# A DLRM tower on one core: ten gathers a chunk in the order of DRAM rows, one transfer out of them, and weights loaded in another order

## The reference, cut to what matters

```python
e = jnp.stack([tbl_0[ids[:, 0]], ..., tbl_38[ids[:, 38]]], axis=1)     # 512 x 39 x 16
z0 = einsum('bid,bjd->bdij', e, e).reshape(B, D, 39 * 39)
cur0 = relu(einsum('bdk,kl->bld', z0, W0))                             # W0: 1521 x 128
next_h, direct0 = split(cur0, 2, axis=1)                               # 64 each
z1 = einsum('bid,bjd->bdij', e, next_h).reshape(B, D, 39 * 64)
cur1 = relu(einsum('bdk,kl->bld', z1, W1))                             # W1: 2496 x 128
z = sum(concatenate([direct0, cur1], axis=1), axis=-1)                 # 512 x 192
h = concatenate([z, dense_ctx], axis=1)                                # 512 x 208
h = maximum(h @ W_top1 + b_top1, 0)
h = maximum(h @ W_top2 + b_top2, 0)
y = h @ W_top3
```

## Time and profile before

| | us |
|---|---|
| median of 3 runs | 443.81 (440.96 to 448.94) |
| profiled execution, its own time | 441.91 |
| its span in the profile | 439.9 |
| matmul busy | 407.8 (93%) |
| VectorE busy | 347.9 (79%) |
| GpSimd busy | 285.5 (65%) |
| ScalarE busy | 225.7 (51%) |

### The profile page before, as it was taken

How to read it: one execution, slowest core, us unless ns; L and a number is a source line. 1 busy time by engine, 2 the same in 40 slices (tenths; PEclk the granted TensorE clock), 3 DMA queues, 4 the chain that set the end, 5 groups by cost and what they waited for, 6 DMA issues and landing times.

```text
span 439.9 us, 4140 instructions
## 1 busy us (share of the span) xinstructions
PE 407.8 (93%) x1490; PEld 250.4 (57%) x1490; DVE 347.9 (79%) x196; ACT 225.7 (51%) x224; POOL 285.5 (65%) x180
## 2 busy tenths in 40 slices
PE   0578699899999999999999999999999999996997
PEld 0444356446566656565756565666656565664564
DVE  0203755799999998989898989898989898999700
ACT  3114345365565647483747474747383747462422
POOL 5787878888888888888888888888888100000000
PEclk9989799999999999999999999999999999999899
DMA  8373629696959495959595977777786858570000
GB/s 282 97 180 76 133 62 217 155 208 153 213 116 213 111 208 112 212 110 216 108 220 120 200 142 171 157 178 153 176 165 157 180 138 197 127 161 0 1 0 2
DMA packets 23988, 64.03 MB, mean 146 GB/s; under 512 B 6755, under 2 KB 14904, under 8 KB 17695
## 3 DMA queue, kind: packets, MB, share of 16 engines
q1 hardware_dynamic: 17620, 60.75, 61.7%
q0 software_dynamic: 5632, 1.35, 3.1%
q10 hardware_dynamic: 715, 1.66, 1.1%
HBM read 59.88 MB, written 3.85 MB: 145 GB/s over the span
## 4 chain that ended last, share of the span: by engine, by line
PE 76%; POOL 12%; issue 5%; DVE 3%; DMA 3%; ACT 0%; DVEq 0%
PE acc L487 15%; POOL found L266 12%; PE acc L519 12%; PE acc L512 11%; PE acc L511 11%; PE acc L530 9%; PE sums L470 6%; PE acc L526 4%; PE spread L500 3%; DVE z_lo L409 3%; DMA found<-in_table_dram,rows_sb 2%; PE spread L559 2%; PE sums L550 1%; DVE z L401 1%; DMA base_sb<-in_base_dram 1%
## 5 line engine op out<-in xcount | busy, mean ns | idle before, releaser
L266 POOL DMA_INDIRECT found<-in_table_dram,rows_sb x176 | 285.3, 1621 | 56.7 <-issue 53.3
L309 ACT ACTIVATE z_hi<-z 128x2048 fp32r<-128x2048 f32 x64 | 122.4, 1912 | 83.1 <-DVE z L401 78.4
L409 DVE TENSOR_TENSOR z_lo<-z,z_hi 128x2048 fp32r<-128x2048 f32 x64 | 146.2, 2286 | 14.6 <-ACT z_hi L309 8.8
L487 PE MATMUL acc<-squares,w 128*128 128x512 f32 (+1 forms) x224 | 111.2, 614 | 0.0
L511 PE MATMUL acc<-z_hi,w_hi 128*128 128x512 f32 x256 | 106.2, 415 | 4.5 <-issue 2.3
L401 DVE TENSOR_TENSOR z<-x_wide,h 128x2048 f32<-128x2048 f32 x48 | 109.6, 2283 | 0.0
L512 PE MATMUL acc<-z_hi,w_lo 128*128 128x512 f32 x256 | 100.2, 391 | 0.0
L401 DVE TENSOR_TENSOR z<-spread,h 128x2048 f32<-128x2048 f32 x32 | 73.2, 2286 | 20.8 <-issue 17.0
L285 ACT ACTIVATE squares<-sums 128x1024 f32<-128x1024 f32 x64 | 58.4, 913 | 59.7 <-PE sums L470 45.7
L519 PE MATMUL acc<-z_lo,w_hi 128*128 128x512 f32 x256 | 83.3, 447 | 1.8 <-DVE z_lo L409 1.8
L519 PEld LDWEIGHTS acc<-z_lo,w_hi 128*128 128x128 f32 x256 | 48.5, 191 | 26.2 <-issue 15.1
(11 more groups left out here) (44 smaller groups left out, 144.5 us busy)
## 6 DMA issues: line engine op xcount, KB each, us to landing
x_wide<-x_rows SPq DMA_DIRECT2D x96, 512.0 KB
x_parts<-x_rows SPq DMA_DIRECT2D x32, 128.0 KB
found<-in_table_dram,rows_sb POOLq DMA_INDIRECT x176
x_rows<-found SPq DMA_DIRECT2D x32, 80.4 KB
w_sb<-in_w_dram SPq DMA_DIRECT2D x1, 1280.0 KB, 6.8
x_rows<-found SPq DMA_DIRECT2D x16, 73.1 KB
z<-in_select_dram ACTq DMA_DIRECT2D x1, 576.0 KB, 7.5
wt_sb<-in_wt_dram SPq DMA_DIRECT2D x1, 512.0 KB
```

The lines of the kernel that those rows point to most:

```text
L266: pool.indirect_dma_start(out=found[:, b, 2, s * D:s * D + D], out_offset=None, in_=table, in_offset=bass.IndirectOffsetOnAxis(ap=rows_sb[ ...
L309: nc.scalar.activation(z_hi[:, n % RING], z[:, n % RING], ACT.Copy).then_inc(hi_done, 1)
L409: nc.vector.tensor_tensor(z_lo[:, n % RING], z[:, n % RING], z_hi[:, n % RING], ALU.subtract).then_inc(lo_done, 1)
L487: last = nc.tensor.matmul(acc0[:, :], w0[rows, t, :], squares[rows, q % RING0, a, :], start=(t == 0), stop=(t == T0 - 1))
```

## The change

The gathered rows are numbered field by field: row f * 32 + b of a chunk, 1248 in all, lies in partition (f * 32 + b) // 10, column (f * 32 + b) % 10. So ten gathers of 125 partitions hold a chunk (GP = 125, SLOTS = 10 for each chunk), and the 125 partitions lie one behind another in DRAM, so that one transfer lays them out. The base values become a table as large as the indices'. Sizes of chunks become lists (SIZES, WIDTH, START), all at their old values. SP loads w0a and mix, which ScalarE's queue did; ScalarE's queue loads w1, which SP's did; the last layers' weights are loaded behind chunk 5's layout. `split(0)` on VectorE stands ahead of w0's sum, on ScalarE ahead of w1's high part; `split(1)` stands ahead of `evict0(0)` on ScalarE and ahead of `multiply(0)` on VectorE. TensorE runs 14 and 5 matmuls of `keep_busy` around the mix instead of 30 behind it, and 12 instead of 14 later; one wait of the dense layers names an earlier multiply.

```diff
-CB = 32
-SETS = 3
-GP = SETS * F
-SLOTS = -(-CB // SETS)
+SIZES = [32] * 16
+GP = 125
+SLOTS = [-(-F * size // GP) for size in SIZES]
+SLOT0 = [sum(SLOTS[:c]) for c in range(CHUNKS)]
...
-        base_sb = sb("base_sb", [GP, 1])
+        base_sb = sb("base_sb", [GP, sum(SLOTS)], I32)
...
             def lay_out(c):
-                b = c % BUFS
+                b, w = c % BUFS, SLOTS[c] * D
                 sp.wait_ge(found_lo_done, c + 1)
-                for s, w in enumerate(SET_COLS):
-                    start = x_rows[b, 0, 0, GW * s:GW * s + 1]
-                    sp.dma_start(bass.AP(start.tensor, start.offset, [[N, F], [FR * N, 3], [1, w]]),
-                                 found[F * s:F * s + F, b, :, 0:w]).then_inc(rows_out[b], 16)
+                start = x_rows[b, 0, 0:1]
+                sp.dma_start(bass.AP(start.tensor, start.offset, [[w, GP], [FR * N, 3], [1, w]]),
+                             found[:, b, :, 0:w]).then_inc(rows_out[b], 16)
...
             sp.dma_start(ids_sb[:, :], ids).then_inc(ids_in, 16)
-            sp.dma_start(w1_sb[:, :, :], w1).then_inc(w1_in, 16)
-            for dst, src in LAYERS:
-                sp.dma_start(dst, src).then_inc(mlp_in, 16)
+            sp.dma_start(w0[:, :, :], w0a).then_inc(w0_in, 16)
+            sp.dma_start(mix_sb[:, :, :], mix).then_inc(mix_in, 16)
             sp.wait_ge(filler_in, 16)
...
                 if c + BUFS < CHUNKS:
                     bring(c + BUFS)
+                if c == 2:
+                    for dst, src in LAYERS:
+                        sp.dma_start(dst, src).then_inc(mlp_in, 16)
...
-                for s in range(SLOTS):
+                for s in range(SLOTS[c]):
+                    i = SLOT0[c] + s
                     pool.indirect_dma_start(
...
-            act.dma_start(w0[:, :, :], w0a).then_inc(w0_in, 16)
             act.dma_start(w0b_sb, w0b).then_inc(w0_in, 16)
-            act.dma_start(mix_sb[:, :, :], mix).then_inc(mix_in, 16)
+            act.dma_start(w1_sb[:, :, :], w1).then_inc(w1_in, 16)
             act.wait_ge(select_in_done, 16)
...
+            split(0)
             act.wait_ge(w1_in, 16)
             nc.scalar.activation(w1_hi[:, :, :], w1_sb[:, 0:VT, :], ACT.Copy).then_inc(w1_hi_ready, 1)
-            split(0)
             for d in range(ND):
                 square(d)
+            split(1)
             evict0(0)
-            split(1)
...
-            nc.vector.tensor_scalar(rows_sb[:, :], ids_sb[:, :], base_sb[:, 0:1], None,
-                                    ALU.add).then_inc(rows_ready, 1)
+            nc.vector.tensor_tensor(rows_sb[:, :], ids_sb[:, :], base_sb[:, :], ALU.add).then_inc(rows_ready, 1)
+            split(0)
             dve.wait_ge(w0_in, 32)
...
             nc.vector.tensor_copy(w0[0:F, 0, :], acc1[0:F, 0:P]).then_inc(w0_ready, 1)
-            split(0)
             dve.wait_ge(w1_hi_ready, 1)
...
             dve.wait_ge(select_ready, 1)
+            split(1)
             multiply(0)
-            split(1)
...
                 if m == 3 and batch == early:
-                    pe.wait_ge(multiplied, G * CHUNKS)
+                    pe.wait_ge(multiplied, G * (CHUNKS - 1) + SPREAD[-1] + 1)
...
+            pe.wait_ge(select_ready, 1)
+            keep_busy(acc0, 14)
             pe.wait_ge(w0_ready, 1)
             pe.wait_ge(mix_in, 16)
...
             last.then_inc(mixed, 1)
-            pe.wait_ge(select_ready, 1)
-            keep_busy(acc0, 30)
+            keep_busy(acc0, 5)
             add_up(0)
...
-            keep_busy(acc1, 14)
+            keep_busy(acc1, 12)
```

More of the change, by code:

```diff
@@ L20 @@
 HALF = 64
-CB = 32
-N = CB * D
-CHUNKS = B // CB
-SETS = 3
-GP = SETS * F
-SLOTS = -(-CB // SETS)
-GW = SLOTS * D
-SET_COLS = [GW, GW, N - 2 * GW]
+SIZES = [32] * 16
+CHUNKS = len(SIZES)
+START = [sum(SIZES[:c]) for c in range(CHUNKS)]
+WIDTH = [size * D for size in SIZES]
+N = max(WIDTH)
+GP = 125
+SLOTS = [-(-F * size // GP) for size in SIZES]
+SLOT0 = [sum(SLOTS[:c]) for c in range(CHUNKS)]
+GW = max(SLOTS) * D
 DENSE = 16
@@ L189, in uses, with gathers @@
             return c // BUFS + 1
+        def gathers(c):
+            return sum(SLOTS[c % BUFS:c + 1:BUFS])
         block = ctx.enter_context(nc.Block())
@@ L469, in add_up @@
                 for a, t in enumerate(DUOS[q % ND]):
-                    last = nc.tensor.matmul(sums[:, a, :], select_sb[:, t, :], x_parts[:, c % BUFS, :],
+                    last = nc.tensor.matmul(sums[:, a, 0:w], select_sb[:, t, :], x_parts[:, c % BUFS, 0:w],
                                             start=True, stop=True)
@@ L486, in contract0 @@
                 for a, t in enumerate(DUOS[d]):
-                    last = nc.tensor.matmul(acc0[:, :], w0[rows, t, :], squares[rows, q % RING0, a, :],
+                    last = nc.tensor.matmul(acc0[:, 0:w], w0[rows, t, :], squares[rows, q % RING0, a, 0:w],
                                             start=(t == 0), stop=(t == T0 - 1))
@@ L499, in spread_out @@
                     rows = slice(32 * q, 32 * q + 32)
-                    last = nc.tensor.matmul(spread[:, q, :], select_sb[rows, T0 + i, :], x_parts[rows, c % BUFS, :],
+                    last = nc.tensor.matmul(spread[:, q, 0:w], select_sb[rows, T0 + i, :], x_parts[rows, c % BUFS, 0:w],
                                             start=True, stop=True)
@@ L631, in layout @@
     tables = [np.ascontiguousarray(inputs[f"tbl_{f}"]) for f in range(F)]
-    by_set = np.zeros((SETS, F, CHUNKS, SLOTS), np.int32)
-    for s, cols in enumerate(SET_COLS):
-        w = cols // D
-        rows = ids.reshape(CHUNKS, CB, F)[:, s * SLOTS:s * SLOTS + w]
-        by_set[s, :, :, 0:w] = rows.transpose(2, 0, 1)
-    starts = np.cumsum([0] + [t.shape[0] for t in tables])[:F].astype(np.float32)
+    starts = np.cumsum([0] + [t.shape[0] for t in tables])[:F].astype(np.int32)
+    by_slot, base = np.zeros((2, GP, sum(SLOTS)), np.int32)
+    for c, size in enumerate(SIZES):
+        cols = slice(SLOT0[c], SLOT0[c] + SLOTS[c])
+        flat, flat_base = np.zeros((2, GP * SLOTS[c]), np.int32)
+        flat[0:F * size] = ids[START[c]:START[c] + size].T.reshape(-1)
+        flat_base[0:F * size] = np.repeat(starts, size)
+        by_slot[:, cols] = flat.reshape(GP, SLOTS[c])
+        base[:, cols] = flat_base.reshape(GP, SLOTS[c])
     from_w0 = np.asarray(inputs["L0_rec_W0"]).reshape(F, F, P)
@@ L676, in layout @@
     return {
[L677 to L678 removed]
+        "ids": by_slot,
+        "base": base,
         "table": np.concatenate(tables),
```

113 lines of the change are left out of this document (61 added, 52 removed).

## The result

The changed kernel takes **444.74 us** (median of 20 runs, 442.31 to 447.81) against 441.87 for the kernel before in the same session (20 runs, 439.83 to 457.15): ratio 1.0081, 95% interval 1.0057 to 1.0104. That is within 2%, but the interval lies above 1: slower, and not faster as forecast. The profiled execution took 444.69 us with a span of 442.8, 2.9 more than before. Executions that ran disturbed (such as the 457.15 of the kernel before) are left out of every ratio, so a ratio is not quite the quotient of the two medians.

The account below looks back on a forecast made before the run. TensorE's matmuls were taken to bound the kernel at 22.88 us a chunk, with only the start movable. TensorE's chain gained 5.9 us, but chunk 3's gathers decided: 442.9 - 4.3 = 438.6 us, range 431.5 to 445.5.

Parts of the forecast that it names:

- Indices: Loads of row numbers and base values at the start: two large loads instead of one and a tiny one, +0.8 us.
- Gathers of chunk 0: GpSimd's gathers at the start: one fewer (-1.30) and w0's sum no longer slowing one (-0.77), -2.07 us.
- Transfer out: Chunk 0's rows sent out after its split: one transfer instead of three, +0.6 us between bounds -0.85 and +2.05.
- h: Chunk 0's h, which allows the first multiply: 0.8 - 2.07 + 0.6 = -0.7 us, first multiply at 39.1.
- The clock and the idle time: TensorE around chunk 1's sums: 2.13 us of idle time and 3.1 us of low clock go, together -5.2 us.
- TensorE's chain: TensorE's work by the time of chunk 2's split: -0.7 - 5.2 = -5.9 us.
- Chunk 2's split: Its gathers land at 50 to 53.5 against a split at 53.5: no wait, but no slack.
- Chunk 3's gathers: Late next, and deciding: landing moves by -4.3 us, ScalarE waits about 6 us ahead of the split, not 4.85.
- A: Rival: index loads and transfer out spread over fewer DMA engines, both upper bounds hold (+2.4, +2.05); 441.7 us, chance 0.26.
- B: Rival: the wait ahead of chunk 3's split goes too, ten gathers landing before ScalarE asks; 433.7 us, chance 0.21.
- C: Rival: fewer warming matmuls let a low clock come elsewhere, so the 3.1 us are lost; 440.2 us, chance 0.12.
- D: Rival: the transfer out goes through so few DMA engines that it bounds every chunk; 486 us, chance 0.04.

Follow-up runs that it names:

- the version with wide loads: The changed kernel with its index and base loads and its transfer out each cut in 120 and 5 partitions, gathers still of 125: 442.89 us, ratio 1.0035.

## Why the prediction was wrong

**The step that failed** is "That 125 rows cost more than 117 would add at most 7% of 10.0 us, 0.7; the row is 1.00 whatever is beside it, so I take 0." The price was bounded by the number of rows, and then put at nothing. It was 1.21 us, 21% more, and does not go by the rows. The prediction had the rule that fits in its hand. The Trainium skill, page "DMA: Bandwidth & Descriptors", section "Why a DMA increments its semaphore by 16 and not by 1", takes the largest number up to 16 that divides the outer dimension on both sides; by it 128, 126, 117, 125, 115 and 127 partitions go to 16, 14, 13, 5, 5 and 1 engines. The issues measured 0.95, 1.00, 1.00, 1.21, 1.19 and 2.55 us: the fewer engines, the longer, and the transfers out likewise. By the same rule each engine gets 8, 9, 9, 25, 23 and 127 rows of a gather, and 0.88 us plus 0.013 us for each of these rows, an estimate fitted to the measured times, meets all six within 0.04 us. The section has an exception for some direct copies that GpSimd issues, 16 engines for any count; the gathers, which are indirect, did not show it, since by it 127 partitions would have cost what 128 do. No trace shows the DMA engines one by one, so that the price goes by this number rests on the six counts. In the prediction the rule was applied to the loads and the transfer out, but not to the gathers, the only ones of which there are 160.

**Step by step.**

- *Indices:* +0.8 forecast, +1.66 measured, within its bounds. At the end it was worth about 1.5 us with 126 partitions, and in the changed kernel, together with the transfer out, up to 2 us by the medians and nothing in the trace (the version with wide loads).
- *Gathers of chunk 0:* -2.07 forecast; from the first issue to the split it is 16.53 us against 16.37, +0.16.
- *Transfer out:* +0.6 forecast, +1.35 measured, within its bounds, and free.
- *h:* -0.7 forecast. The split that h now waits behind came at 42.15, not 37, since its gathers were late, and the first multiply was at 43.74, not 39.1. "Cost 0, cover about 1 us" failed with the cover, by the price of ten more gathers; 1.3 us of it is the split's place (42.40 with it back).
- *The clock and the idle time:* half right. TensorE had no idle time ahead of chunk 1's sums, and from the second sum over that chunk (53.40) to the spread (57.96) it was 4.56 us instead of 7.49, 2.9 gained against 3.1 forecast. But a low stretch came earlier instead, behind the 5.47 us of idle time that end at 48.12, and from the first multiply (+3.9) to chunk 0's whole group (+0.2) 3.7 us were gained, not 5.2.
- *TensorE's chain:* -5.9 forecast, +0.2 measured, h's +3.9 less the 3.7. ScalarE was to reach chunk 3's split at 68.7 and reached it at 74.75, and chunk 1's wide transfers, put 5.3 us earlier, were issued at 65.50, 1.4 later than in the earlier trace rows. With 126 partitions both were nearly met (69.47, and 58.71). This second miss need not have cost anything: the gathers landed 8.9 us after ScalarE was there.
- *Chunk 2's split:* no wait, as forecast.
- *Chunk 3's gathers:* rightly named as what decides. The fortieth's issue was to end at 67.7 to 68.1 and ended at 75.45: 0.9 of it the indices, about 4.8 the price of the 39 before it (67.33 us for them, 62.5 forecast), 1.7 its own slow issue, held up by VectorE. The landing was to move by -4.3 and moved by +4.47.
- *Last layers' loads, w0's and w1's order, the tail, the period:* nothing, as forecast. The steps stay at 22.86 across the last layers' loads (issued from 134.62).

**The rivals.** A, narrow transfers, was the right rule in two harmless places: with both of its prices real the forecast of 441.7 still missed the third. B's second stall grew instead. C's mechanism came, a low stretch elsewhere; with 126 partitions doing away with it gave 0.75 us at chunk 1's whole group. D's mechanism shows with 127 partitions, one engine by the rule (17.92 us out to place in chunk 0, and the largest part of the chain), not with 125. The range, to 445.5, held the time only because of A's margin. What the change's idea is worth with a fitting number shows at 126: 1.3% less, near the forecast's 1.0% (438.6 against 442.9). That is in part luck, since there the indices and the transfer out cost nothing (+0.03 and -0.18 us, not +0.8 and +0.6).

## What to carry to other kernels

Choose the number of partitions of a gather, a load or a transfer out for its divisors before its rows: 126 in place of 125 was worth 9 us here, 7 of them by the gathers, and 127, one run, cost 270. Where two chains meet at one wait (here TensorE's and GpSimd's at chunk 3's split), work out both arrival times; what the earlier one gains is only idle time. Such a price is to be measured with one row of the very shape, not bounded by its size.

## What the runs showed of the hardware

VectorE's operations that read two operands from SBUF hold GpSimd's gathers up: an issue of 1.00 us takes 4.69 beside two of them and 9.09 beside four, and stays at 1.00 beside one that reads an operand from PSUM (78.94 above). Where the gathers fall among them changes with small shifts. The changed kernel with the transfer out in two had its fortieth gather issued at 71.70 without such a hold-up and landed at 80.70 in its profiled execution, 2.9 us ahead of the changed kernel's, though the price of its gathers is the same. So a few us between two profiled executions at this place prove little by themselves.

The last step, from chunk 14's whole group to chunk 15's, was about 21.9 or 23.5 us in all kernels but one (25.3 with 126 partitions and chunk 3's split later). TensorE idles for a part of it (busy 1.81 us in 404 to 408 in the kernel before), and in some the granted clock falls behind that. The kernel before (step 23.47), and the same with chunk 1's split ahead (21.88), in 408 to 412:

```profile
408.00:412.00 4.00, 4.00 (x8) 1.82 (x6) 4.00 (x3) 2.92 (x2) 0.00 (x0) 0.58 0.00 0
```

```profile
408.00:412.00 4.00, 4.00 (x12) 1.79 (x11) 4.00 (x3) 3.56 (x2) 0.00 (x0) 1.00 0.00 0
```

These kernels have the same code at the end, and differ there by 1.6 us; each was profiled once, so whether two executions of one kernel do is not shown. The changed kernel's had the short step: the 4.75 us that it lost by chunk 1's whole group (95.97 against 91.22 in the earlier trace rows) ended as 2.9 of span, which flatters it by 1.6.
